# Filling the unused rows of the expert pages block by block, by copies in memory, in one attention, shared-FFN and MoE kernel

## The chip, the cores and the metric

One core of a Trainium2 chip runs the whole program. The metric is the device time of one execution in microseconds, as the median of several executions. The engines are TensorE (PE, with its weight loads PEld), VectorE (DVE), ScalarE (ACT), GpSimd (POOL) and SyncE (SP); transfers are issued by SP and POOL and carried out by 16 DMA engines.

## What is computed

The reference, cut to what matters (4096 tokens of width 512, all float32):

```
x = x + layernorm(linear_attention(layernorm(x), w_qkv, b_qkv, w_out, b_out))   # 16 heads, chunks of 128, decaying state
h = layernorm(x)
probs = softmax(h @ router.T); top 2 of 8 experts, weights renormalised
moe    = sum over e of combine[:, e] * (silu(h @ gate_e.T) * (h @ up_e.T)) @ down_e.T     # inner width 352
shared = sigmoid(h @ shared_gate.T) * ((silu(h @ g.T) * (h @ u.T)) @ d.T)                 # inner width 1408
out = x + layernorm(moe + shared)
```

The kernel computes only the two chosen experts of each token. It gathers tokens by expert for that.

## The kernel before, in words

**Stages.** The 4096 tokens are 8 blocks (`NB`) of 512 (`TOK`), each of 4 chunks (`NC`) of 128 rows. Phase 1 (to about 1360 us) runs attention, normalisation and routing of block after block and puts the shared FFN of earlier blocks between its pieces. Phase 2 (to about 1970 us) runs the experts. Phase 3 runs the last block of the shared FFN and the final normalisation. Matrix products are done as three passes on split operands (high and low parts), by the helper `three` (L728 to L730).

**Expert pages.** Tokens go to memory as rows of `xs_d` (`x1_normed_by_expert`): 39 pages (`NG`) of 256 rows (`GT`), each row 514 float32 (`DX`), 2056 bytes: the 512 normalised values, the combine weight and the token's number. A page belongs to one expert and is opened when a block needs it, so pages are used in order of time. The rows of a page that no token takes must hold an unused row: zeros, weight 0 and the number of a spare row. These patterns lie in two SBUF tiles `unused_row`, which are `xn2[:, 2]` and `xn2[:, 3]`, the same memory that later holds the normalised chunks 2 and 3 of each block.

**The fill before.** POOL issues 13 pieces `("zf", 0, i)` in block 0, each of 3 pages as two transfers (L563) from `unused_row`. Each piece first waits until TensorE has done the score product S of chunk i // 4, group i % 4. The first piece also clears a tail of `ffn_out` (L560). Two places wait for all the fills: the scatter `("sc", 0)` on POOL, and the ScalarE piece `("LX", 0, 1)` (L970), which overwrites the SBUF tiles.

**The scatter.** In each block a, after the routing ranks are known (piece RK), POOL issues 8 indirect transfers (L581) that put 128 rows each at their places in `xs_d`. Phase 2 gathers 128 rows at a time from it (L597).

**What sets the order.** Pieces of each block have hand-set places in `PLACES` and `OPENING`; block a adds `PERIOD` (44) times a, and `attention_offsets` returns them. `schedule` sorts them and puts the parts of the shared FFN between them: from place 60 on (`FILL_FROM`) each placed piece adds `max(1, passes)` to what was given, and an FFN part goes in whenever what was given lies behind an aim that grows evenly with the place. Each engine then runs its own pieces of this one list in order (`ORDER`), and waits on counters of finished pieces of the others. SP issues in order too: it loads `x` for the residual (xr, L665), attention weights (wa, L678), shared-FFN weights (raw, L690) and the transposed activations (xti, L700). POOL issues the stores x1o (L568, into `out`), xto (L572), sho (L592), and the scatter. xr for chunk 2 waits for the store x1o of chunk 0, since they share a tile.

Of the kernel before, what the change touches and what calls it, by code (L numbers as in the profile page):

```python
# [16 lines left out]
P = 128  # L17
# [4 lines left out]
G = HEADS // GH  # L22
TOK = 512
NC = TOK // P
NB = 8
SEQ = 1024
NCH = NB * NC
E, I_MOE, I_SH = 8, 352, 1408
# [14 lines left out]
GT = 256  # L43
NG = (2 * NB * TOK + E * (GT - 1)) // GT
SUB = GT // P
# [3 lines left out]
PART = [s for g in range(NG) for s in range(SUBS[g])]  # L49
FULLS = [sum(n == SUB for n in SUBS[:g]) for g in range(NG + 1)]  # L50
NJ = len(GROUP)
NZ = NG // 3
ZROWS = NG * GT // NZ
GU = 2 * I_MOE
DT = 3
DROWS = (P, P, I_MOE - 2 * P)
# [7 lines left out]
DX = D + 2  # L64
# [66 lines left out]
def attention_offsets(a):  # L131

    s = []
    for kind, places in PLACES.items():
        if a == 0:
            places = OPENING.get(kind, places)
        if a == 0 and kind == "xto":
            continue
        shape = ARGS.get(kind, (len(places),) if len(places) > 1 else ())
        for args, at in zip(itertools.product(*(range(n) for n in shape)), places):  # L140
            s.append((at, (kind, a, *args)))
    if a == 0:
        for i in range(NZ):
            s.append((20 + 8 * (i // G) + i % G, ("zf", a, i)))
    return s


# [91 lines left out]
def schedule():  # L239
# [70 lines left out]
    for q in range(LAST, NCH):  # L310
# [14 lines left out]
ORDER = {e: [p for p in PIECES if e in PARTS[p[0]]] for e in "PAVSG"}  # L325
PLACE = {e: {p: i + 1 for i, p in enumerate(ORDER[e])} for e in "PAV"}
# [32 lines left out]
def build(nc, x, w_att, w_ffn, w_gu, w_dn, w_router, b_qk, b_v, b_out, t_mask, t_dq, t_dk, t_lam, t_blk, t_ident,  # L359
# [6 lines left out]
    xs_d = nc.dram_tensor("x1_normed_by_expert", [NG * GT, DX], F32, kind="Internal").ap()  # L366
# [3 lines left out]
    with ExitStack() as ctx:  # L370
# [3 lines left out]
        def sem(name):  # L374
            return ctx.enter_context(nc.semaphore(name))
# [27 lines left out]
        def ffn_small(scope, tag):  # L403
# [18 lines left out]
        xin = sb("x_in", [NC, D], scope=phase1)  # L422
# [36 lines left out]
        cnt, pages, new, cum, page_end, page_base, away, fresh, had, had_end = (sb(n, [E], scope=phase1) for n in (  # L459
            "count", "pages", "pages_new", "pages_cum", "page_end", "page_base", "page_away", "page_fresh", "pages_had",  # L460
            "pages_had_end"))
# [6 lines left out]
        unused_row = [xn2[:, 2 + i, :] for i in range(SUB)]  # L468
# [56 lines left out]
        xt_out = sem("xT_out")  # L525
        xt_in = [sem(f"xT_in{k}") for k in range(KT)]
        xt_used = sem("xT_used")
        xs_zero, acc_zero, unused_id = sem("x1_by_expert_zero"), sem("ffn_out_zero"), sem("unused_row_id")
        second_weight = sem("second_weight")
        xs_out = [sem(f"x1_by_expert_out{i}") for i in range(NC)]  # L530
        sh_out = [sem(f"shared_out{i}") for i in range(2)]
# [20 lines left out]
        def pool_piece(pool, kind, *args):  # L552
            if kind == "zf":
                a, i = args
                pool.wait_ge(p_piece, done("P", "S", a, *divmod(i, G)))
                if i == 0:
# [1 line left out]
                    pool.wait_ge(unused_id, SUB)  # L558
                    tail = acc_d[(NB - 1) * TOK:, :].rearrange("(n p) d -> p n d", p=P)
                    pool.dma_start(out=tail, in_=unused_row[0][:, 0:D].unsqueeze(1).to_broadcast([P, NC + SUB, D])).then_inc(acc_zero, 16)  # L560
                rows = xs_d[i * ZROWS:(i + 1) * ZROWS, :].rearrange("(n s p) d -> s p n d", p=P, s=SUB)
                for k in range(SUB):
                    pool.dma_start(out=rows[k], in_=unused_row[k].unsqueeze(1).to_broadcast([P, ZROWS // GT, DX])  # L563
                                   ).then_inc(xs_zero, 16)
            elif kind == "x1o":
                a, c = args
                pool.wait_ge(v_piece, done("V", "L", a, c // 2))
# [6 lines left out]
            elif kind == "sc":  # L574
                a, = args
                pool.wait_ge(v_piece, max(done("V", "RK", a), done("V", "SM4", a)))
                if a == 0:
                    pool.wait_ge(xs_zero, 16 * SUB * NZ)
                for k in range(2):
                    for c in range(NC):  # L580
                        pool.indirect_dma_start(  # L581
# [356 lines left out]
        def act_attention(act, piece):  # L938
# [11 lines left out]
            elif kind == "N1":  # L950
                c, = args
                act.wait_ge(v_piece, done("V", "N1B", a))
                op = act.activation(xin[:, c, :], xin[:, c, :], ACT.Identity, bias=nshift[:, c:c + 1],
                                    scale=nrstd[:, c:c + 1])
            elif kind == "LN":
                h, = args
                act.wait_ge(v_piece, done("V", "LO", a, h))
                for i in range(2):
                    op = act.activation(o[:, i, :], o[:, i, :], ACT.Identity, bias=oshift[:, i:i + 1],
                                        scale=orstd[:, i:i + 1])  # L960
            elif kind == "LX":
                h, = args
                act.wait_ge(v_piece, done("V", "L", a, h))
                if (a, h) == (0, 1):
                    act.wait_ge(acc_zero, 16)
                    act.wait_ge(xs_zero, 16 * SUB * NZ)
                for i in range(2):
                    if a:
                        act.wait_ge(xs_out[2 * h + i], 32 * a)
                    op = act.activation(xn2[:, 2 * h + i, 0:D], x1[:, i, :], ACT.Identity, bias=lshift[:, i:i + 1],  # L970
                                        scale=lrstd[:, i:i + 1])
            elif kind == "W":
                u, = args
                act.wait_ge(wr_in[u % WAR], 16 * (u // WAR + 1))
                if u >= WAS:
                    act.wait_ge(p_piece, done("P", *last_use(a, u - WAS)))
                    act.wait_ge(ws_out[u % WAS], 32 * (u // WAS))
                op = act.copy(wa_hi[:, u % WAS, :], wa_raw(u))
            elif kind == "QK":
                m, = args  # L980
                dst = qT if m < G else kT
                if a and m == 0:
                    act.wait_ge(p_piece, done("P", "S", a - 1, NC - 1, G - 1))
                    act.wait_ge(v_piece, done("V", "KT", a - 1, NC - 1))
                op = act.activation(dst[:, m % G, :], b, ACT.Identity, bias=bqk[:, m:m + 1])
            elif kind == "Z":
                c, g = args
                if (c, g) == (0, 0):
                    act.wait_ge(a_piece, done("A", "QK", a, G - 1))
                if 4 * c + g >= 2:  # L990
                    act.wait_ge(p_piece, done("P", "S", a, *divmod(4 * c + g - 2, G)))
                for j in range(GH):
                    r = slice(j * HD, (j + 1) * HD)
                    op = act.copy(qz[r, g % 2, j, :], qT[r, g, c * P:(c + 1) * P])  # L994
            elif kind == "IP":
                c, half = args
                if half == 0 and c > 0:
                    act.wait_ge(p_piece, done("P", "OUT", a, c - 1))
                elif half == 0 and a:
                    act.wait_ge(p_piece, done("P", "OUT", a - 1, NC - 1))  # L1000
                op = act.copy(oT_hi[:, 2 * half:2 * half + 2, :], chunked(b[:, 0:2 * P]))  # L1001
            elif kind == "R1":
                op = act.copy(lgT[0:2 * R, :], b[0:2 * R, :])
            elif kind == "SM1":
                act.wait_ge(v_piece, done("V", "SM1", a))
                act.activation(sm["z"][:, :, :], lg[:, :, E:R], ACT.Exp, scale=-1.0)
                op = act.activation(sm["e"][:, :, :], sm["d"][:, :, :], ACT.Exp)
# [611 lines left out]
```

## Time and profile before

| | |
|---|---|
| median of 3 runs | 2072.4 us (2069.81 to 2073.74) |
| the profiled execution's own time | 2071.72 us |
| its span in the profile | 2069.9 us |
| PE busy / PEld busy | 1924.6 us (93%) / 1560.1 us (75%) |
| DVE / ACT / POOL busy | 1212.6 / 960.5 / 433.8 us |
| DMA | 389.26 MB, mean 188 GB/s |
| chain that ended last | PE 57%, DVE 6%, DMA 3%, ACT 2% |

The profile gives the span of one execution; 1.8 us of its time lie around the span. The chain that ended last is followed back from the last instruction. PE takes by far the most of it, so the places where PE stands idle, and for whom, decide what an edit outside PE is worth.

### The profile page before, as it was taken

To read this page: it belongs to the slowest core of one execution; us is meant where nothing else is said; L and a number is where in the kernel's file an instruction comes from. 1 tells how busy PE (TensorE), PEld (TensorE's weight loads), DVE (VectorE), ACT (ScalarE), POOL (GpSimd) and SP (SyncE) were. 2 spreads that over 40 slices of the span, in tenths; PEclk is the share of its full clock that TensorE was granted. 3 is DMA by queue.
4 is the path that set the end of the run, shared out by engine and by line. 5 is a ranking of instruction groups with operands and counts; after the bars stand their busy time and mean duration, and the time that the engine had idled before them with its cause. 6 is when DMAs were issued, how large, how long until landed. Compare 5 with 4: busy or idle time off the path is not lost.

```text
span 2069.9 us, 28246 instructions
## 1 busy us (share of the span) xinstructions
PE 1924.6 (93%) x10000; PEld 1560.1 (75%) x10000; DVE 1212.6 (59%) x2874; ACT 960.5 (46%) x1928; POOL 433.8 (21%) x444
## 2 busy tenths in 40 slices
PE   6788999899989999999999999999999999999996
PEld 5566677677767777767777777777998989899875
DVE  4555664574665574574575555664666666666466
ACT  4333343443443443443354334344666666666453
POOL 2301001001001001101000100120455555555222
PEclk9889999999999999999999999999999999999999
DMA  8976246336246337326435334565888988888597
GB/s 279 365 253 207 64 133 231 118 106 224 93 156 208 113 109 242 132 96 214 156 106 199 131 120 143 166 224 173 220 245 247 249 245 239 258 239 244 121 274 179
DMA packets 138378, 389.26 MB, mean 188 GB/s; under 512 B 16944, under 2 KB 17088, under 8 KB 131328
## 3 DMA queue, kind: packets, MB, share of 16 engines
q0 software_dynamic: 50256, 204.91, 33.4%
q1 hardware_dynamic: 87552, 182.49, 27.0%
q8 instruction: 81, 1.33, 0.3%
q14 instruction: 57, 0.47, 0.1%
q10 hardware_dynamic: 432, 0.07, 0.0%
HBM read 281.87 MB, written 105.53 MB: 187 GB/s over the span
## 4 chain that ended last, share of the span: by engine, by line
PE 57%; DVE 6%; DMA 3%; ACT 2%; issue 2%; SPq 1%; POOL 1%; DVEq 0%; ACTq 0%; POOLq 0%
PE banks L728 17%; PE banks L730 16%; PE banks L729 16%; PE banks L795 2%; PE banks L916 1%; DMA moe_dn_raw<-w_dn,w_index 1%; PE banks L922 1%; DMA xT_lo<-xt_scratch 1%; PE banks L809 1%; PE banks L802 1%; PE banks L815 1%; DMA ffn_w_raw<-w_ffn 1%; DVE ffn_gate_up_lo L1376 0%; PE banks L761 0%; SPq L700 0%
## 5 line engine op out<-in xcount | busy, mean ns | idle before, releaser
L728 PE MATMUL banks<-xT_hi,ffn_gate_up_hi 128*128 128x512 f32 x704 | 297.9, 423 | 14.6 <-DMA xT_lo<-xt_scratch 6.2
L730 PE MATMUL banks<-xT_hi,ffn_gate_up_lo 128*128 128x512 f32 x704 | 278.7, 396 | 0.0
L729 PE MATMUL banks<-xT_lo,ffn_gate_up_hi 128*128 128x512 f32 x704 | 278.2, 395 | 0.0
L728 PE MATMUL banks<-moe_gu_hi,moe_xT_hi 128*128 128x352 f32 x592 | 204.8, 346 | 3.0 <-DVE moe_xT_lo L1400 3.0
L994 ACT COPY q_one_head<-qT 32x128 f32<-32x128 f32 x512 | 151.0, 295 | 104.2 <-PE banks L795 98.9
L1393 DVE TENSOR_TENSOR moe_gu_lo<-moe_gu_raw,moe_gu_hi 128x704 fp32r<-128x704 f32 x156 | 135.3, 887 | 97.7 <-ACT moe_gu_hi L1051 97.7
L730 PE MATMUL banks<-moe_gu_hi,moe_xT_lo 128*128 128x352 f32 x592 | 191.2, 323 | 0.0
L729 PE MATMUL banks<-moe_gu_lo,moe_xT_hi 128*128 128x352 f32 x592 | 190.5, 322 | 0.0
L728 PEld LDWEIGHTS banks<-xT_hi,ffn_gate_up_hi 128*128 128x128 f32 x704 | 134.8, 191 | 59.9 <-issue 12.7
L633 POOL DMA_INDIRECT ffn_out<-moe_y,moe_x x74 | 119.2, 1610 | 201.0 <-ACT moe_y L1077 201.0
L729 PEld LDWEIGHTS banks<-xT_lo,ffn_gate_up_hi 128*128 128x128 f32 x704 | 135.0, 192 | 31.6 <-issue 6.7
L730 PEld LDWEIGHTS banks<-xT_hi,ffn_gate_up_lo 128*128 128x128 f32 x704 | 134.3, 191 | 29.7
L1376 DVE TENSOR_TENSOR ffn_gate_up_lo<-ffn_w_raw,ffn_gate_up_hi 128x768 fp32r<-128x768 f32 (+1 forms) x176 | 120.7, 686 | 57.6 <-ACT ffn_gate_up_hi L1024 57.4
L568 POOL DMA_DIRECT2D out<-x x32 | 17.5, 552 | 595.5 <-DVE x_shift L1116 595.2
L728 PE MATMUL banks<-ffn_down_hi,hidden_hi 128*128 128x512 f32 x308 | 132.8, 431 | 4.0 <-DVE hidden_lo L1386 3.9
L1001 ACT CAST attT_hi<-banks 128x256 fp32r<-128x256 f32 x64 | 23.6, 369 | 240.3 <-PE banks L809 240.2
L795 PE MATMUL banks<-q_one_head,kT 128*128 128x512 f32 x256 | 131.9, 609 | 0.7 <-ACT q_one_head L994 0.6
L1397 DVE TENSOR_TENSOR moe_dn_lo<-moe_dn_raw,moe_dn_hi 128x512 fp32r<-128x512 f32 x117 | 77.2, 689 | 93.7 <-ACT moe_dn_hi L1057 93.5
L730 PE MATMUL banks<-ffn_down_hi,hidden_lo 128*128 128x512 f32 x308 | 120.8, 392 | 0.0
L729 PE MATMUL banks<-ffn_down_lo,hidden_hi 128*128 128x512 f32 x308 | 120.2, 390 | 0.0
L581 POOL DMA_INDIRECT x_normed_by_expert<-x_normed,pos_int x64 | 65.9, 1029 | 249.2 <-DVE pos_int L1345 230.9
L1051 ACT CAST moe_gu_hi<-moe_gu_raw 128x704 fp32r<-128x704 f32 x156 | 118.1, 781 | 0.0
(273 smaller groups left out, 4408.1 us busy)
## 6 DMA issues: line engine op xcount, KB each, us to landing
ffn_w_raw<-w_ffn SPq DMA_DIRECT2D x176, 384.0 KB, 3.2
att_w_hi<-att_w_split SPq DMA_DIRECT2D x112, 256.0 KB, 3.7
att_w_lo<-att_w_split SPq DMA_DIRECT2D x112, 256.0 KB, 4.5
x_normed_by_expert<-x_normed POOLq DMA_DIRECT2D x26, 771.0 KB, 18.2
x_in<-x SPq DMA_DIRECT2D x32, 256.0 KB, 4.8
x<-x SPq DMA_DIRECT2D x32, 256.0 KB, 5.4
out<-x POOLq DMA_DIRECT2D x32, 256.0 KB, 2.7
fin_ffn_out<-ffn_out SPq DMA_DIRECT2D x32, 256.0 KB, 8.5
```

The lines of the kernel that those rows point to most:

```text
L581: pool.indirect_dma_start(out=xs_d[:, :], out_offset=bass.IndirectOffsetOnAxis(ap=posi[:, NC * a + c, k:k + 1], axis=0), in_=xn2[:, c, :], ...
L633: pool.indirect_dma_start(out=acc_d[:, :], out_offset=bass.IndirectOffsetOnAxis(ap=xg[:, j % XG, D + 1:DX].bitcast(I32), axis=0), in_=y[:, ...
L728: pe.matmul(out_ap, l_hi, r_hi, start=start, stop=False)
L729: pe.matmul(out_ap, l_hi, r_lo, start=False, stop=False)
L730: return pe.matmul(out_ap, l_lo, r_hi, start=False, stop=stop)
L795: mm = pe.matmul(b, kT[:, g, c * P:(c + 1) * P], qz[:, g % 2].rearrange("p h t -> p (h t)"), start=True, stop=True)
L994: op = act.copy(qz[r, g % 2, j, :], qT[r, g, c * P:(c + 1) * P])
L1001: op = act.copy(oT_hi[:, 2 * half:2 * half + 2, :], chunked(b[:, 0:2 * P]))
L1051: op = act.copy(gu_hi[:, i % 2, k, :], rgu[:, i % 2, k * GU:(k + 1) * GU])
L1376: op = ve.tensor_tensor(wgu_lo[:, n % WGU, gu_cut], src, wgu_hi[:, n % WGU, gu_cut].bitcast(F32), ALU.subtract)
L1393: op = ve.tensor_tensor(gu_lo[:, i % 2, k, :], rgu[:, i % 2, k * GU:(k + 1) * GU], gu_hi[:, i % 2, k, :].bitcast(F32), ALU.subtract)
L1397: op = ve.tensor_tensor(dn_lo[:, i % 2, k, :], rdn[:, k * D:(k + 1) * D], dn_hi[:, i % 2, k, :].bitcast(F32), ALU.subtract)
```

## The change

All 39 pages are no longer filled in block 0. Block 0 fills 12 of them from SBUF: the last page (38), which serves as the pattern, and pages 0 to 10. `PAGES[a]` is the number of pages that can be open after block a: 11, 15, 19, 23, 27, 31, 35, 38. Each later block a gets one new POOL piece `("zc", a)` at place 50, which issues a single transfer within memory: page 38, repeated, to the pages from `PAGES[a-1]` to `PAGES[a]` (4 pages; 3 in block 7). The scatter of block a waits for it. The fill pieces are 5 now, at places 20, 24, 28, 32 and 36, and piece i waits for the score product i as before.

```
-NZ = NG // 3
-ZROWS = NG * GT // NZ
+PAGES = [min(NG - 1, ((a + 1) * 2 * TOK + E * (GT - 1)) // GT) for a in range(NB)]
+FILLS = [range(NG - 1, NG)] + [range(q, min(q + 3, PAGES[0])) for q in range(0, PAGES[0], 3)]
...
     if a == 0:
-        for i in range(NZ):
-            s.append((20 + 8 * (i // G) + i % G, ("zf", a, i)))
+        for i in range(len(FILLS)):
+            s.append((20 + 4 * i, ("zf", a, i)))
+    else:
+        s.append((50, ("zc", a)))
...
-                rows = xs_d[i * ZROWS:(i + 1) * ZROWS, :].rearrange("(n s p) d -> s p n d", p=P, s=SUB)
+                rows = xs_d[FILLS[i][0] * GT:(FILLS[i][-1] + 1) * GT, :].rearrange("(n s p) d -> s p n d", p=P, s=SUB)
                 for k in range(SUB):
-                    pool.dma_start(out=rows[k], in_=unused_row[k].unsqueeze(1).to_broadcast([P, ZROWS // GT, DX])
+                    pool.dma_start(out=rows[k], in_=unused_row[k].unsqueeze(1).to_broadcast([P, len(FILLS[i]), DX])
                                    ).then_inc(xs_zero, 16)
+            elif kind == "zc":
+                a, = args
+                if a == 1:
+                    pool.wait_ge(xs_zero, 16 * SUB * len(FILLS))
+                pages = PAGES[a] - PAGES[a - 1]
+                rows = xs_d[PAGES[a - 1] * GT:PAGES[a] * GT, :].rearrange("(n r) d -> n r d", r=GT)
+                pool.dma_start(out=rows, in_=xs_d[(NG - 1) * GT:, :].unsqueeze(0).to_broadcast([pages, GT, DX])).then_inc(xs_copied, 16)
...
                 if a == 0:
-                    pool.wait_ge(xs_zero, 16 * SUB * NZ)
+                    pool.wait_ge(xs_zero, 16 * SUB * len(FILLS))
+                else:
+                    pool.wait_ge(xs_copied, 16 * a)
...
                 if (a, h) == (0, 1):
                     act.wait_ge(acc_zero, 16)
-                    act.wait_ge(xs_zero, 16 * SUB * NZ)
+                    act.wait_ge(xs_zero, 16 * SUB * len(FILLS))
```

## Rows read from the trace of the kernel before

**Rows 1.** The page: span and engine totals.

```profile
span 2069.9 us, 28246 instructions
PE 1924.6 (93%) x10000; PEld 1560.1 (75%) x10000; DVE 1212.6 (59%) x2874; ACT 960.5 (46%) x1928; POOL 433.8 (21%) x444
```

**Rows 2.** Windows of the opening: busy by engine, PEclk, DMA share, GB/s.

```profile
45.00:107.00 62.00, 48.17 (x267) 32.87 (x268) 36.13 (x89) 23.38 (x69) 20.45 (x29) 0.89 1.03 365
...
107.00:125.00 18.00, 13.73 (x89) 10.10 (x87) 12.58 (x36) 6.70 (x15) 0.50 (x1) 0.91 0.97 342
```

**Rows 3.** Waits of PE over the whole run: us, times, longest.

```profile
PE banks L802 <- DVE probsT L1245: 32.7, 14, 5.1
...
PE banks L728 <- DMA xT_lo<-xt_scratch: 6.2, 10, 2.7
```

**Rows 4.** The fill line L563: issue time in ns, first and last start, landing.

```profile
L563 POOL DMA_DIRECT2D x_normed_by_expert<-x_normed x26: 744/756/763, 45.4 to 106.7; - x26
...
DMA to landing us min/median/max: 12.0/18.2/22.0
```

**Rows 5.** POOL's timeline in the opening: start, us, operation, idle before.

```profile
99.41 1.11 POOL L568 DMA_DIRECT2D out<-x  x2
```

**Rows 6.** SP's timeline and SP's waits in the opening.

```profile
69.22 52.86 SPq L665 DMA_DIRECT2D x<-x  x4
...
SPq L665 <- DMA out<-x: 21.8, 2, 21.5
```

**Rows 7.** Timelines of DVE, ACT and PE where fills could be waited for.

```profile
92.65 1.29 DVE L1271 TENSOR_TENSOR x<-projected,x 128x512 f32<-128x512 f32 x2 [0.88 <-ACT projected L959]
...
130.65 1.30 DVE L1271 TENSOR_TENSOR x<-projected,x 128x512 f32<-128x512 f32 x2 [0.38 <-ACT projected L959]
...
136.13 1.51 ACT L970 ACTIVATE x_normed<-x,x_shift,x_rstd 128x512 f32<-128x512 f32 x2
...
66.46 1.01 PE L802 MATMUL banks<-q_decayed,state 128*128 128x128 f32 x4 [4.57 <-DVE probsT L1245]
130.41 0.77 PE L728 MATMUL banks<-x_normedT_hi,att_w_hi 128*128 128x512 f32 x1 [5.17 <-DVE x_normedT_lo L1224]
```

**Rows 8.** POOL's timeline where the copies will stand.

```profile
248.88 1.16 POOL L568 DMA_DIRECT2D out<-x  x2 [55.67 <-DVE x_shift L1116]
...
338.58 1.45 POOL L581 DMA_INDIRECT x_normed_by_expert<-x_normed,pos_int  x1 [25.54 <-DVE pos_int L1345]
...
602.58 0.54 POOL L592 DMA_DIRECT2D ffn_out<-shared_staged  x1 [0.29 <-ACT shared_staged L1043]
627.35 1.07 POOL L568 DMA_DIRECT2D out<-x  x2 [24.24 <-DVE x_shift L1116]
...
1246.47 0.54 POOL L592 DMA_DIRECT2D ffn_out<-shared_staged  x1 [1.54 <-ACT shared_staged L1043]
...
1299.53 1.46 POOL L581 DMA_INDIRECT x_normed_by_expert<-x_normed,pos_int  x1 [28.48 <-DVE pos_int L1345]
```

**Rows 9.** Windows behind copies 1 and 3 (columns as rows 2).

```profile
249.00:291.00 42.00, 40.54 (x225) 31.79 (x226) 27.05 (x61) 20.17 (x44) 1.04 (x2) 0.96 0.26 82
...
603.00:645.00 42.00, 38.53 (x175) 31.31 (x176) 21.66 (x60) 16.91 (x29) 2.26 (x5) 0.96 0.66 221
```

**Rows 10.** Loads of shared-FFN weights: SP and ACT timelines, and the page's landing.

```profile
253.43 6.96 SPq L690 DMA_DIRECT2D ffn_w_raw<-w_ffn  x2
...
269.24 0.41 ACT L1021 CAST ffn_gate_up_hi<-ffn_w_raw 128x256 fp32r<-128x256 f32 x1
...
ffn_w_raw<-w_ffn SPq DMA_DIRECT2D x176, 384.0 KB, 3.2
```

**Rows 11.** Weights of block 4's first product: load, landing, first use.

```profile
614.55 0.33 SPq L678 DMA_DIRECT2D att_w_hi<-att_w_split  x1
...
att_w_lo<-att_w_split SPq DMA_DIRECT2D x112, 256.0 KB, 4.5
...
L728 PE MATMUL banks<-x_normedT_hi,att_w_hi x32: 392/396/505, 621.3 to 650.3; 128*128 128x512 f32 x32
```

More of the change, by code:

```diff
@@ L527, in build @@
         xt_used = sem("xT_used")
-        xs_zero, acc_zero, unused_id = sem("x1_by_expert_zero"), sem("ffn_out_zero"), sem("unused_row_id")
+        xs_zero, xs_copied, acc_zero, unused_id = sem("x1_by_expert_zero"), sem("x1_by_expert_copied"), sem("ffn_out_zero"), sem("unused_row_id")
         second_weight = sem("second_weight")
```

2 rows, old and new, of the table PARTS are left out of this document.

## The prediction

> **What bounds the kernel now.** I first read the page's totals: PE is busy for 1924.6 of 2069.9 us, 93% [rows 1]. So an edit to transfers pays only where it shortens one of PE's idle stretches, and costs only where it makes one. The sum below is made against this execution: 2069.9 us of span and 1.8 us around it, 2071.7; the median of the runs shown is 0.7 above that.
>
> Next I read the windows of the opening. From 45 to 107 us the DMA share is 1.03 at 365 GB/s, and it stays at 0.97 to 125 us [rows 2]: the 39 pages are poured out here and every other transfer queues with them. In the same window PE is busy for 48.2 of 62 us. It looks as if the fills starve it. The list of PE's waits decides that: PE waits mostly for VectorE's masked probabilities (32.7 us in 14 waits), and the only transfer that it names is the transposed activations, 6.2 us in 10 waits [rows 3], none of them before 370 us. So I looked behind VectorE and ScalarE for a hidden transfer, below.
>
> **Part 1: fewer fills in block 0.** 26 transfers of 384 rows become 10: two of 128 rows, six of 384, two of 256. The removed pages are 39 - 12 = 27. A page is 256 x 2056 B = 0.526 MB, so 14.2 MB leave the opening; at 365 GB/s that is 39 us of full DMA. On POOL 26 x 756 ns = 19.7 us of issuing [rows 4] fall to at most 10 x 756 ns = 7.6 us, and POOL stands idle around them, so that is worth nothing by itself. The first 12 pages still wait for the products S of chunk 0 and the first of chunk 1, as they did, so the queues are full until about 75 us and much emptier after that. What was late because of it:
> - The store x1o of chunk 0 is issued at 99.41 [rows 5]. SP's next residual load waits for it, for 21.5 us [rows 6], which is landing behind the queued fills. That will shrink to a few microseconds, since nothing is queued ahead of the store any more. Who waits for SP there? VectorE's residual sum of the second pair starts at 130.65, and the row says that ScalarE's normalised projection released it, not the load [rows 7]. Gain 0.
> - The residual loads of the first pair, issued at 69.22 [rows 6], take up to 21.8 us, to about 92; the sum that reads them starts at 92.65, released by ScalarE [rows 7]. It is covered by about half a microsecond only. Gain 0, and a margin becomes large.
> - ScalarE's L970 at 136.13 must wait for all fills. The last was issued at 106.7 and lands at most 22 us later [rows 4], by 129; the row shows no idle time before it [rows 7]. Gain 0.
> - PE's idle stretches of 4.6 us before 66.46 and 5.2 us before 130.41 [rows 7] end on VectorE, which was at work on split weights and on the statistics of a normalisation.
>
> The bound from one side is 0. From the other, if these stretches were transfers after all: 4.6 + 5.2 = 9.8 us. I take 0, since each releaser named has just finished in its row.
>
> **Part 2: seven copies in memory.** Copies 1 to 6 write 4 pages, 2.1 MB, copy 7 writes 3. They write 14.2 MB in all, so nothing is saved in bytes written, and as much is now read from memory too. On POOL the issue cost is bounded by rows of the same kind: 756 ns for 384 rows [rows 4], 555 ns each for 128 rows [rows 5], so about 0.8 ns a row more and 1.3 us for 1024 rows, at most 2 us if it goes as whole fills (1024/384 x 756 ns). Seven times 1.3 us is 9 us on an engine with 50 us of idle time at each of these places [rows 8]. Cost 0.
>
> How long a copy runs has no row. The nearest is the fill, with the same row size and target: 2.1 MB at 365 GB/s [rows 2] is 5.8 us. If reading from memory costs as much again, 11.5 us. Those are the ends when all 16 engines share it; on four engines they are 23 and 46 us. I take 23 us for the reason given in the second rival.
>
> What each length meets:
> - The scatter waits for the copy. Copy 1 is issued at 249.9 and the scatter at 338.58: 88 us. The tightest is copy 7, 1247.0 to 1299.53: 52 us [rows 8]. Even 46 us fits.
> - POOL's transfers queued behind it: after copy 1 the next stands more than 50 us later. Behind copy 3 (issued at 603.1) the store x1o follows at 627.35 [rows 8], just past 23 us. Its reader is SP's residual load of the next block, some 50 us later. Copy 1's own wait for the fills is met by 129 us.
> - Shared-FFN weight loads run beside every copy. One issued at 253.43 is used at 269.24, 15.8 us later, and lands in 3.2 us [rows 10]. Twice or three times 3.2 us is still covered. DMA share behind copy 1 is 0.26 [rows 9], so there is room.
> - Attention weights of block 4 stand behind copy 3, where the share is already 0.66 [rows 9]. The pair is issued at 614.55 and 614.92, lands 4.5 us later, at 619.4, and PE uses it at 621.3 [rows 11]. Margin 1.9 us: this is the only thin cover that I found, and all other copies lie away from such loads. I take +0.5 us.
>
> **Part 3: the order.** The copy piece stands at places 94 and more, past the point where the FFN's planner counts, and adds one pass each time. Worked through the planner's rule, this moves ten pieces, among them ST of chunks 1 and 3 in block 3, one score product in block 6 and the down products 20, 27 and 40; each goes one FFN part (12 passes of some 0.24 us, 2.8 us) earlier or later. PE's work is the same. The bound for all is some 4 us either way, about one of the longer waits for the masked probabilities [rows 3]; value 0.
>
> **Sum.** 2071.7 + 0 (opening) + 0.5 (copy 3) + 0 (order), about 2072.
>
> **The rivals.**
>
> *The opening was bound by transfers (faster).* For it: the queues were full for 80 us, two covers there are as thin as half a microsecond, and the opening's PE is the idlest of phase 1. Against it: no releaser is a transfer. If a third to all of the 9.8 us come back, it gives 2062 to 2068; I put it at 2067. A lucky shift of the order ends there too. Chance 0.17.
>
> *Copy 3 takes the weights of block 4 (slower).* The transfer's outermost dimension is the 4 pages, not 128 partitions as in the fills. If the engines are dealt out along it, four of 16 carry a page each for 23 us or more, and any load spread over all 16 ends when those four let it. Place: 614.55 to 621.3, eight loads of 256 KB [rows 11]. Alone they need 2.1 MB at 365 GB/s, 5.8 us; on engines shared by halves 11.5 us, so the last comes 5.8 us later and the first by about 1.5. Price: up to 5.8 less the margin of 1.9, about 4 us, and some 4 more if at 46 us the copy also meets the loads after 627. It decides if copy 3 still runs 11.5 us after its issue. Result 2076 to 2080; with the spread of the order, 2077. Against it: later loads have their own margins, and it happens once. Chance 0.14.
>
> The Trainium skill, page "DMA: Bandwidth & Descriptors", section on why a DMA increments its semaphore by 16, says that the number of DMA engines is the largest one up to 16 that divides the slowest dimension of both sides, and its rules for kernel authors warn of a leading zero-stride broadcast of c copies, which keeps a transfer on at most c engines. By it each copy runs on four engines (three in block 7). No row of this trace shows such a shape. With copies of 23 us by it the sum stays 2072; with 5.8 us, for all 16 engines, it would be 2071.7.
>
> *The change does not do what it says.* The copies could run longer than 52 us (for example on one engine: 2.1 MB at 23 GB/s, 92 us), so that the scatter and POOL behind it wait. The scatter's landing is needed again only by the next block's normalised rows and, in block 7, by phase 2 near 1360 us. That gives 2072 to 2090. Chance 0.03.
>
> **How the numbers follow.** About 0.2%, or 4 us, is what a measurement of this kernel can tell from no change. Forecast, no visible change: 0.66. Slower by more: 0.14 + 0.03 = 0.17. Faster by more: 0.17. The forecast's own range is 2068 to 2076. The range 2066 to 2078 takes in the milder half of both rivals.
>
> **What would show it.** Right if the profile after has 10 transfers at L563's line instead of 26, a DMA share from 80 to 125 us well below 1, SP's wait of 21.5 us gone, and still the same PE stretches before 66.5 and 130.4 us and phase 2 at the same time. The copy's landing tells the engines: 6 to 12 us for 16, 23 to 46 for four. The first rival is right if PE starts block 1's first product well before 130 us. The second is right if PE's waits show attention weights near 621 us. I would be wrong altogether if a shared-FFN weight load or a scatter shows up as a releaser on PE's path.

## Result, and the profile after

The changed kernel takes 2095.6 us (median of 5 runs, 2093.36 to 2100.43), the kernel before 2073.6 us beside it (5 runs): ratio 1.0107, 95% interval 1.0093 to 1.0121. It is 22 us slower, where 2072 was forecast and 2078 was the upper end. The profiled execution is the longest of the five (2100.43 us), so its trace shows some 5 us more than the median.

The page after, span and engine totals, against [rows 1]:

```profile
span 2098.6 us, 28244 instructions
PE 1934.7 (92%) x10000; PEld 1567.6 (75%) x10000; DVE 1213.2 (58%) x2874; ACT 960.5 (46%) x1928; POOL 426.5 (20%) x435
```

The span grew by 28.7 us and PE's busy time by 10.1, with as many instructions; the rest is new idle time.

**The opening is as forecast.** The windows of the opening after (same columns as [rows 2]), SP's wait for the store, and the two PE stretches of [rows 7]:

```profile
45.00:107.00 62.00, 47.26 (x259) 33.03 (x259) 33.91 (x84) 21.34 (x62) 8.50 (x13) 0.86 0.68 237
107.00:125.00 18.00, 13.72 (x83) 9.77 (x82) 13.54 (x39) 8.49 (x21) 0.00 (x0) 0.91 0.00 0
```

```profile
SPq L676 <- DMA out<-x: 1.5, 2, 1.0
```

```profile
66.40 1.19 PE L813 MATMUL banks<-q_decayed,state 128*128 128x128 f32 x4 [4.57 <-DVE probsT L1256]
...
132.65 0.77 PE L739 MATMUL banks<-x_normedT_hi,att_w_hi 128*128 128x512 f32 x1 [5.17 <-DVE x_normedT_lo L1235]
```

The DMA share falls from 1.03 to 0.68 and from 0.97 to nothing. SP's longest wait for the store falls from 21.5 us to 1.0. And PE stands idle for the same 4.57 and 5.17 us. The transfers were not what it waited for.

**The copies run as long as forecast.** The copy line L573, the page's issues, and the DMA queues in the window from 262 to 272 us, in the middle of copy 1 (queue and kind: packets, MB, share of 16 engines; POOL's transfers are q0, SP's q1):

```profile
L573 POOL DMA_DIRECT2D x_normed_by_expert<-x_normed_by_expert x7: 657/684/684, 252.2 to 1268.7; - x7
...
DMA to landing us min/median/max: 24.4/24.7/25.8
```

```profile
q0 software_dynamic: 30, 0.99, 22.9%
q1 hardware_dynamic: 354, 0.77, 22.1%
```

A copy lands after 24.7 us; 23 was taken. q0's share of 22.9% of 16 engines is 3.7 engines: the copy is on four. By this the rule of the Trainium skill that the prediction weighed, on how many engines a transfer gets (page "DMA: Bandwidth & Descriptors", section on why a DMA increments its semaphore by 16), agrees with the trace. A packet of the copy is 0.99 MB / 30 = 33 KB, which is 16 rows of 2056 bytes (32,896): the rows of a page are contiguous and were joined. Each of the four engines carries a page, 16 such runs.

**The loads beside the copies are where it failed.** SP and PE at copy 3 (timeline columns as in [rows 5]), and the issues of the window from 600 to 626 us:

```profile
606.70 0.68 POOL L573 DMA_DIRECT2D x_normed_by_expert<-x_normed_by_expert  x1
...
616.70 0.33 SPq L689 DMA_DIRECT2D att_w_hi<-att_w_split  x1
617.07 0.43 SPq L689 DMA_DIRECT2D att_w_lo<-att_w_split  x1
...
633.12 0.76 PE L739 MATMUL banks<-x_normedT_hi,att_w_hi 128*128 128x512 f32 x1 [9.54 <-DMA att_w_lo<-att_w_split]
```

```profile
x_normed_by_expert<-x_normed_by_expert POOLq DMA_DIRECT2D x1, 2056.0 KB, 24.5
...
att_w_lo<-att_w_split SPq DMA_DIRECT2D x4, 256.0 KB, 17.3
```

The weights of block 4, which landed in 4.5 us [rows 11], take 17.3. The copy ends at 606.7 + 24.5 = 631.2. The low half of the first pair, issued at 617.07, lands 15.8 us later, at 632.9, and PE, idle for 9.5 us, starts at 633.12. The stall costs more than its length. These are the window of 42 us from copy 3 on, against [rows 9], and the first 5.7 us after the stall:

```profile
607.00:649.00 42.00, 27.00 (x117) 21.23 (x116) 20.46 (x57) 14.58 (x26) 1.51 (x3) 0.88 0.53 187
...
633.10:638.80 5.70, 5.68 (x14) 4.44 (x14) 0.00 (x0) 0.19 (x1) 0.00 (x0) 0.50 0.26 100
```

PE's granted clock is 0.50 in the second row, the lower of its two levels (1.2 GHz), after the 9.5 us in which it did nothing. Its 14 products there start 0.43 us apart, those behind 639 us 0.235 apart: another 2.7 us, 12.2 in all.

The waits of PE and of ScalarE over the whole run (us, times, longest):

```profile
PE banks L813 <- DVE probsT L1256: 36.2, 15, 5.0
...
PE banks L739 <- DMA att_w_lo<-att_w_split: 9.5, 1, 9.5
PE banks L739 <- DVE state L1267: 8.6, 5, 2.6
...
PE banks L843 <- DVE xT_staged_lo L1235: 5.7, 1, 5.7
```

```profile
ACT ffn_gate_up_hi L1032 <- DMA ffn_w_raw<-w_ffn: 16.6, 7, 7.2
ACT ffn_gate_up_hi L1035 <- DMA ffn_w_raw<-w_ffn: 14.0, 6, 5.1
```

ScalarE's 30.6 us were 13.4 before (7.1 in 3 waits and 6.3 in 5). Between 1060 and 1380 us, where copies 6 and 7 stand, they are 17.2 us after and 0.4 before. Where PE's path shifts is read from POOL's xto stores, one in each block, and the first gather of expert weights. Their start, less that in the kernel before, in us:

| block | 1 | 2 | 3 | 4 | 5 | 6 | 7 | phase 2 |
|---|---|---|---|---|---|---|---|---|
| changed kernel | +2.7 | +2.5 | +14.6 | +14.6 | +15.1 | +25.0 | +27.3 | +29.5 |
| order alone (e2) | 0.0 | -0.1 | -1.2 | -1.2 | -1.4 | +4.1 | +5.3 | +6.0 |
| copies alone, four engines (e3) | +2.3 | +2.1 | +11.7 | +11.7 | +11.8 | +17.2 | +18.9 | +22.5 |
| copies alone, 16 engines (e12) | -1.5 | -1.8 | -1.8 | -1.7 | -1.8 | -1.2 | -2.7 | -0.2 |

Two steps: 12 us at block 3, the stall and the slower clock behind it, and 10 at block 6. The same kernel run twice (e6 and e12) differs by up to 3 us in such a row, so smaller shifts say nothing.

### The profile page after: what moved, and what is told of

The parts are those of the page before. It is cut to its first block, busy times and chain, and to the rows that moved or that the text cites. A ratio compares the mean times of both kernels' runs of the same rounds, so it can differ in the third digit from the quotient of the medians.

```text
span 2098.6 us, 28244 instructions
## 1 busy us (share of the span) xinstructions
PE 1934.7 (92%) x10000; PEld 1567.6 (75%) x10000; DVE 1213.2 (58%) x2874; ACT 960.5 (46%) x1928; POOL 426.5 (20%) x435
## 4 chain that ended last, share of the span: by engine, by line
PE 76%; DVE 11%; DMA 6%; ACT 3%; issue 3%; SPq 1%; POOL 1%; DVEq 0%; ACTq 0%; POOLq 0%
PE banks L739 21%; PE banks L741 20%; PE banks L740 20%; PE banks L806 4%; DMA xT_lo<-xt_scratch 2%; DMA ffn_w_raw<-w_ffn 2%; PE banks L820 2%; PE banks L826 2%; PE banks L813 1%; PE banks L927 1%; DMA moe_dn_raw<-w_dn,w_index 1%; DVE probsT L1256 1%; PE banks L933 1%; DVE pair_stats L1133 1%; PE banks L772 1%
## 5 line engine op out<-in xcount | busy, mean ns | idle before, releaser
L577 POOL DMA_DIRECT2D out<-x x32 | 17.9, 561 | 627.9 <-DVE x_shift L1127 627.9
L739 PE MATMUL banks<-x_normedT_hi,att_w_hi 128*128 128x512 f32 x256 | 106.4, 415 | 19.7 <-DMA att_w_lo<-att_w_split 9.5
## 6 DMA issues: line engine op xcount, KB each, us to landing
x_normed_by_expert<-x_normed_by_expert POOLq DMA_DIRECT2D x6, 2056.0 KB, 24.6
```

Source lines behind the costliest of these rows:

```text
L739: pe.matmul(out_ap, l_hi, r_hi, start=start, stop=False)
```

## The experiments

All are timed against the kernel before on the same chip (its medians there: 2074.3, 2074.0, 2073.4, 2074.0 and 2075.0). All seven copies stand where the change put them unless it is said otherwise. "Old order" means that the planner doesn't count the copy pieces, so that the rest of the list is that of before.

| | median us | ratio | 95% interval |
|---|---|---|---|
| e1 changed order, 16 engines, runs of 4112 B | 2076.7 | 1.0015 | 1.0004 to 1.0026 |
| e2 kernel before with the changed order | 2079.6 | 1.0024 | 1.0010 to 1.0039 |
| e3 old order, copies as changed | 2090.7 | 1.0080 | 1.0061 to 1.0099 |
| e4 old order, 16 engines, 4112 B | 2076.5 | 1.0012 | 1.0000 to 1.0024 |
| e5 old order, two copies of half rows | 2078.2 | 1.0023 | 1.0012 to 1.0035 |
| e6 old order, 16 engines, 32,896 B | 2070.0 | 0.9982 | 0.9970 to 0.9995 |
| e7 old order, as changed, at place 30 | 2191.1 | 1.0567 | 1.0543 to 1.0591 |
| e8 old order, 16 engines, 4112 B, at place 30 | 2116.7 | 1.0208 | 1.0188 to 1.0228 |
| e9 old order, columns split 512 + 2 | 2080.8 | 1.0040 | 1.0026 to 1.0054 |
| e10 changed order, 16 engines, 32,896 B | 2076.2 | 1.0005 | 0.9993 to 1.0017 |
| e11 e12, with all 39 pages filled in block 0 too | 2072.1 | 0.9996 | 0.9987 to 1.0005 |
| e12 e6 once more | 2072.5 | 1.0000 | 0.9989 to 1.0012 |
| e13 old order, two copies at each place | 2096.2 | 1.0113 | 1.0091 to 1.0134 |
| e14 e12's shape, two copies at each place | 2076.9 | 1.0013 | 1.0002 to 1.0024 |
| e15 changed kernel, copy 3 alone on 16 | 2088.0 | 1.0068 | 1.0051 to 1.0085 |
| e16 changed kernel, all but copy 3 on 16 | 2089.4 | 1.0075 | 1.0062 to 1.0088 |
| e17 old order, copies twice as long on four | 2159.5 | 1.0407 | 1.0387 to 1.0427 |

**Order against shape: e1 to e4.** The edits, alone or together:

```
-            given += max(1, passes([piece]))                       # old order; the same in the total
+            given += 0 if piece[0] == "zc" else max(1, passes([piece]))
...
-                rows = xs_d[...].rearrange("(n r) d -> n r d", r=GT)      # four engines
+                rows = xs_d[...].rearrange("(n p s) d -> p n (s d)", p=P, s=GT // P)
+                page = xs_d[(NG - 1) * GT:, :].rearrange("(p s) d -> p (s d)", s=GT // P)
+                pool.dma_start(out=rows, in_=page.unsqueeze(1).to_broadcast([P, pages, GT // P * DX])).then_inc(xs_copied, 16)
```

e2 is the kernel before, with empty copy pieces that are counted.

> The changed kernel with the same seven copies, but with 128 as the outermost dimension of both sides, as the fills have it. Theory A (few engines: a copy sits on four of 16 for 24.6 us, and every load that is spread over 16 lands only when those four let it): a copy lands in 6 to 12 us, the stall of 9.5 us before block 4's first product is gone, and the time falls from 2095.6 to 2074 to 2080. Theory B (the planner's shifted order): 2090 to 2096 still, since the order is the changed one. Theory C (traffic within memory slows the loads whatever engines carry it): a copy of some 10 us, 2085 to 2095.

> The kernel before with all 39 pages filled in block 0, plus the seven pieces at place 50, which issue nothing: the planner's order is that of the changed kernel, and nothing else is. Theory A: 2072 to 2077, the order costs at most a few microseconds. Theory B: 2085 to 2095.

> The changed kernel with its copies as they are, but the planner does not count them, so all other pieces stand as in the kernel before. Theory A: 2090 to 2096, all or nearly all of the loss is still there. Theory B: 2073 to 2078.

> Both mended: copies over 16 engines and the planner's old order. Theory A: 2071 to 2076, level with the kernel before, because the opening was not bound by its transfers. If the opening relief were worth something after all: below 2069.

Measured: the same bytes to the same places in the same order cost 18.9 us more in the changed shape (2095.6 against 2076.7 for e1; in the old order 2090.7 against 2076.5). The landing of a copy falls from 24.6 us to 11.8 (e1), that of the residual loads that start some 11 us behind its issue from 14 or 15 us to 4.2 (e4), since the copy is then all but over. The order has a price of its own: e2 against before 5 us, the changed kernel against e3 4.9 us; but e1 against e4, the same pair of orders with 16 engines, shows 0.2. By the table of shifts e2 loses it in block 6. PE's waits between 985 and 1112 us in e2 hold two that the kernel before lacks in that block:

```profile
PE banks L804 <- DVE probsT L1247: 2.6, 1, 2.6
...
PE banks L797 <- ACT shared_staged L1045: 1.4, 1, 1.4
```

So a piece moved by one FFN part uncovers chains on VectorE and ScalarE that the FFN hid. The shape makes most of the loss, the order at most the rest.

**Engines or length of a run: e5, e6 and e9.** e6 takes `p=16` in place of `p=P`, so that 16 engines carry runs of 32,896 bytes. e5 and e9 split the columns, so that rows aren't contiguous and can't be joined:

```
+                page = xs_d[(NG - 1) * GT:, :].unsqueeze(0).to_broadcast([pages, GT, DX])
+                for cols in (slice(0, DX // 2), slice(DX // 2, DX)):      # e9: slice(0, D), slice(D, DX)
+                    pool.dma_start(out=rows[:, :, cols], in_=page[:, :, cols]).then_inc(xs_copied, 16)
```

> Planner's old order, copies still on four engines (the pages outermost), but in two transfers of half rows, 1028 B a piece, so that contiguous rows can't be merged into long runs. In the changed kernel a page of 526,336 B in 24.6 us on one engine is 16 runs of 32,896 B of 1.54 us each, if rows are merged. Theory A1 (few engines: whatever lies behind the copy on the four engines waits for it): copy 25 to 30 us, 2088 to 2092 as in the run with four engines and the old order. Theory A2 (long runs: an engine serves the queues in turn, one run against one row of 2 KB, so a load with 8 rows per engine waits 8 x 1.54 = 12.3 us): residual loads beside a copy land in 4 to 8 us instead of 14, and the time is 2075 to 2079.

> Planner's old order, the same runs of 32,896 B as in the changed kernel, but 16 of them outermost, so that each engine carries four. Theory A1: a copy lands in 6 to 12 us, 2075 to 2079. Theory A2: the same copy length, and a load beside it waits at most for four runs, 6 us, so 2075 to 2079 as well; only loads that stand within 6 us of the copy's issue land late, in 8 to 10 us.

> Old order, four engines, copies split by columns: one transfer with rows of 2048 B (the 512 values) and one with the last two columns, 8 B a row. The run with half rows put its two transfers on the engines side by side and a load beside them still landed with the copy's end, so it left open whether length of run or number of engines holds the loads. Here nearly all bytes are in one transfer on four engines. Theory A1 (whatever lies behind or beside the copy on those engines comes out with the copy's end, whatever its runs): main copy 24 to 30 us, residual loads beside it 13 to 16 us, time 2086 to 2092. Theory A2 (turns between queues, one long run against one short row): residual loads 4 to 8 us, time 2075 to 2080.

e6 says that long runs by themselves cost nothing at this place: a copy is over in 10.2 us, four runs an engine. Its lead over before did not hold in e12 (1.0000), so I take it as chance. e5 lies between and decides less: its two halves go side by side (q0 is at 48.5% of 16 engines between 416 and 426 us, so on eight), residual loads land in 9.9 us, the weights of block 4 in 14.0, and PE stands 5.9 us at 626.9. (The row of that stall names VectorE, but the low half of the first pair, issued at 614.5, lands 12.1 us later, at 626.6.) e9 did not make the shape that it was meant to: the page's issues give

```profile
x_normed_by_expert<-x_normed_by_expert POOLq DMA_DIRECT2D x6, 2048.0 KB, 10.3
...
x_normed_by_expert<-x_normed_by_expert POOLq DMA_DIRECT2D x6, 8.0 KB, 32.0
```

2 MB in 10.3 us are not four engines' work, although the pages are outermost here too, and why is not shown; but the 8 KB of the last two columns, 1024 rows of 8 bytes, take 32 us, and loads beside them are late (residual 9.1 us, weights 13.5). It says how dear tiny rows are, nothing on the question, which e5 and e9 leave open.

**Another place: e7 and e8.** The copy piece at place 30 in place of 50, on four engines and on 16.

> Planner's old order, copies as in the changed kernel, but at place 30 of each block instead of 50, so that copy 3 runs before and not beside the load of block 4's attention weights. If the loss was mostly that one meeting: the 7.8 us stall before block 4's first product is gone and the time falls from 2090.7 to 2078 to 2083; what is left is late shared-FFN weights. If every copy costs about the same wherever it stands: 2088 to 2093.

> Planner's old order, 16 engines with runs of 4112 B, at place 30. Both theories: level with the same kernel at place 50, 2072 to 2077. Below 2071 only if the opening relief pays and the 2 us that are left at place 50 come from where the copies stand.

Both missed, far on the other side. POOL issues the copy right behind the scatter, at 193.9, and SP issues the eight loads of the output weights from 195.0 on, in every block. PE's waits in e7 and in e8:

```profile
PE banks L739 <- DMA att_w_lo<-att_w_split: 107.5, 6, 19.9
```

```profile
PE banks L740 <- DMA att_w_lo<-att_w_split: 34.8, 6, 6.7
```

That is one meeting with a weight load, measured six times: 17.9 us of PE with the copy on four engines and 5.8 us on 16. The expectation had looked at POOL's idle time there, not at what SP loads next.

**The opening and the whole: e10, e11 and e12.** e10 is the changed kernel with e6's copy, e12 is e6 again. e11 adds to e12 all fills of before in block 0:

```
-FILLS = [range(NG - 1, NG)] + [range(q, min(q + 3, PAGES[0])) for q in range(0, PAGES[0], 3)]
+FILLS = [range(q, q + 3) for q in range(0, NG, 3)]
```

> The changed kernel with nothing else mended than the copy's shape (16 runs of 32,896 B per page outermost). If order and copy add up: the fastest form so far, 2070, plus what the shifted order costs, 2 to 5 us: 2072 to 2075. If 16 engines with 4112 B are as good: 2076 as that run gave.

> Old order, all 39 pages filled in block 0 as in the kernel before, and the seven copies on 16 engines with long runs as well (they write the same again). Against the same kernel with 12 pages filled this leaves only the relief of the opening. If the relief is worth nothing, as predicted: 2069 to 2074, level within 2 us with the kernel beside it. If it is worth something: 3 to 10 us slower than that.

> The same kernel as the one with 16 engines and long runs before, beside the two above: again 2068 to 2073, slightly below the kernel before; if the lead was chance, 2073 to 2077.

e11 and e12 differ by 0.4 us: fewer fills in block 0 are worth nothing that shows. Only the copy's shape mended (e10) gives 19.4 of the 22 us back; mended in the order of before (e12) it is level with the kernel before, and no kernel beats that in each of its runs.

**Copy 3 by itself: e15 and e16.** The copy takes one shape for `a == 3`, the other for the rest.

> The changed kernel with copy 3 alone spread over 16 engines, the other six as they were. If the stall on block 4's weights is what copy 3 costs, some 12 us come back of 2095.6: 2083 to 2085, and what is left (some 8 us over 2076.2) lies at copies 6 and 7. If most of the loss comes from the shared-FFN weights at all copies, less than 4 us come back: 2092 or more.

> The complement: the changed kernel with the other six copies spread over 16 engines and copy 3 alone on four. If copy 3 costs 12 us by itself: 2076.2 + 12, 2087 to 2089. If the loss is spread over all copies: 2076 to 2080.

Alone on four engines, copy 3 costs 2089.4 - 2076.2 = 13.2 us, as expected. Alone mended it gives back 7.6 of the 19.4 (each median is good to some 3 us), less than the 12 expected and more than the 4 of the other case. The shifts at block 3 are clear (+11.2 in e16, +2.4 in e15); what follows in e15 is a wait of 6.2 us for VectorE's transposed activations and ScalarE's waits of 32.5 us for shared-FFN weights, 17.3 of them between 1060 and 1380 us, at copies 6 and 7. So copy 3 is the largest single part, some 8 to 13 us, and the other six cost 6 to 12 together.

**Turns, or held until the end: e13, e14 and e17.** The loads beside a copy landed near its end, so either an engine serves the queues in turns, with a load's rows between long runs, or a load waits until the copy is over. e13 and e14 issue a second copy, to the pages of the next block, right behind the first. e17 keeps one transfer but makes it twice as long, with two pattern pages and

```
+                m = 2 if a < NB - 2 else 1
+                rows = xs_d[PAGES[a - 1] * GT:(PAGES[a - 1] + m * pages) * GT, :].rearrange("(n r) d -> n r d", r=m * GT)
+                pool.dma_start(out=rows, in_=xs_d[(NG - m) * GT:, :].unsqueeze(0).to_broadcast([pages, m * GT, DX])).then_inc(xs_copied, 16)
```

> The old order, and at each of the seven places two copies on four engines, the second to the pages of the next block (none in block 7), so that those engines are busy for about 49 us in place of 24.6. A load that starts some 13 us into the first copy lands 14 to 15 us later with one copy. Theory A, an engine takes a run of each queue in turns: such a load has the same few rows to bring past the same long runs, so it still lands in 14 to 16 us, though copies go on for 35 us more; only the loads between 25 and 49 us are late in addition. Theory B, a load is held until the copies issued before it are done: it lands in 35 to 38 us. Time: A 2093 to 2110, B above 2120.

> The same doubled copies, but spread over all 16 engines (runs of 32,896 bytes), so some 20 us in place of 10. Theory A and B alike: each load that meets them is late by up to 10 us more than beside a single copy; both copies are over before or just as the loads that start 13 us later need their engines. 2072 to 2082. Above 2085 would say that the bytes copied, not the four engines, make the loss.

> The old order and one copy at each place, but copies 1 to 5 write eight pages, four destinations of two pages each, from two pattern pages: the outermost dimension is still 4, so four engines should carry 32 long runs each, some 49 us in place of 24.6 (two separate copies had gone to different engines side by side). Theory A, turns between long runs and a load's own rows: a residual load that starts 13 us into the copy still lands in 14 to 16 us, and the shared-FFN weights that start 4 us into it in 16. Theory B, held until the copy is over: 35 to 38 us and 45 us. Time: A 2095 to 2120, since the loads of the next 25 us are late too, B above 2130.

e13 did not do what it was to do. Its queues between 262 and 272 us:

```profile
q0 software_dynamic: 60, 1.97, 46.4%
```

Twice the packets and twice the share of the changed kernel (30 and 22.9%), 7.4 engines: the second copy ran on other engines beside the first, and both were over within 27 us. Loads beside them landed as before (residual 14.6 to 15.9 us), which fits both theories. e14's time came as expected: twice the bytes on 16 engines, the two copies over some 18 us after they are issued, cost 2.9 us. So it is not the bytes. But its loads are late too, as its issues from 413 to 425 and from 262 to 275 us show:

```profile
ffn_w_raw<-w_ffn SPq DMA_DIRECT2D x2, 384.0 KB, 16.4
...
x<-x SPq DMA_DIRECT2D x2, 256.0 KB, 9.9
```

Long runs on 16 engines hold up a load as those on four do, while they last. Four engines make one copy last 24.6 us in place of 10, and the loads that start 10 us and more into it, block 4's weights above all, then still meet it.

e17 tells the two apart. SP's timeline beside copy 1, which POOL issues at 251.66, and ScalarE's waits for the weights:

```profile
255.09 6.93 SPq L702 DMA_DIRECT2D ffn_w_raw<-w_ffn  x2
262.12 0.85 SPq L677 DMA_DIRECT2D x<-x  x2
271.20 4.24 SPq L702 DMA_DIRECT2D ffn_w_raw<-w_ffn  x2
```

```profile
270.86 0.41 ACT L1033 CAST ffn_gate_up_hi<-ffn_w_raw 128x256 fp32r<-128x256 f32 x1
...
283.38 0.83 ACT L1036 CAST ffn_gate_up_hi<-ffn_w_raw 128x768 fp32r<-128x768 f32 x1 [1.32 <-DMA ffn_w_raw<-w_ffn]
...
299.27 0.40 ACT L1033 CAST ffn_gate_up_hi<-ffn_w_raw 128x256 fp32r<-128x256 f32 x1 [12.82 <-DMA ffn_w_raw<-w_ffn]
```

The landings of the loads one by one, from the issues of narrow windows (issue plus landing), the copy ending at 251.7 + 46.2 = 297.9:

| load | issued | landed | after the one before |
|---|---|---|---|
| shared-FFN weights | 255.1 | 270.7 | |
| shared-FFN weights | 261.7 | 283.4 | 12.7 |
| residual x, first | 262.1 | 294.9 | 11.5 |
| residual x, second | 262.6 | 298.3 | 3.4 |
| shared-FFN weights | 271.2 | 299.3 | 1.0 |

A load held until the copy is over could not land at 270.7 and 283.4. In turns it can, and the queues in the window from 282 to 286 us show the turns themselves (packets, MB, share of 16 engines):

```profile
q0 software_dynamic: 13, 0.43, 24.8%
q1 hardware_dynamic: 13, 0.02, 1.5%
```

There are thirteen runs of the copy and thirteen packets of SP's loads. Taken one by one, each of the four engines sends one packet of a load (0.08 to 0.12 us for a row) and then one run of the copy (0.248 x 16 x 4 us / 13 = 1.22 us), over and over, 1.30 to 1.34 us a turn. A load of 128 rows puts 8 rows on each engine, and behind them the trace has a packet of 4 bytes that takes a turn as well. On the last of the four engines this packet goes at 270.34, 282.87 and 294.45, right before the landings at 270.7, 283.4 and 294.9. Nine turns are 11.7 to 12.1 us; the distances measured are 12.7 and 11.5. As soon as the copy ends, the rest lands within 1.4 us.

So each load needs nine turns, and loads queue behind each other. The first shared-FFN weights, with nothing ahead of them, landed in 15.6 us, as theory A had it (16). The residual loads took 33 to 36 us, which is what theory B had given (35 to 38), because the weights ahead of them used up most of the copy's 32 turns. The time, 2159, is above both 2120 and 2130: a long copy builds a backlog, and the weights of block 4 in its path stop PE for 28.3 us at once. Neither the residual loads nor the time tell the theories apart; the two landings during the copy and the turns one by one do. The expectation for turns left the backlog out.

The Trainium skill, page "DMA: Bandwidth & Descriptors", section "Queues, rings and completion order", says that a DMA engine goes round the queues that have work for it and changes only when a whole packet is through. e17's trace agrees: its turns change at each packet, and the distances of 11.5 and 12.7 us follow from them. It also says that a packet holds several descriptors. e5's trace agrees: its rows of 1028 bytes go in packets of 4112, 0.165 us each. But nine turns of such a packet and a row of a load are 2.3 us, too little for residual loads of 9.9 us, so why short rows delay loads as well is not shown.

## Why the prediction was wrong

Its forecast, no visible change, is out. The terms of the sum that failed are those of the copies: +0.5 us for copy 3, and nothing for the shared-FFN weights beside the others. The second rival, "Copy 3 takes the weights of block 4", had the place and the four engines right, but a chance of 0.14 and a price of 4 us.

- *What bounds the kernel; the opening, value 0.* Right. SP's wait went, the PE stretches stayed, and e11 against e12 is level. The first rival ("bound by transfers") falls with it.
- *The copies: 23 us, four engines; POOL's issue and the scatter's cover, cost 0.* Right: 24.7 us on 3.7 engines, 0.68 us an issue; no scatter waits on PE's path.
- *"Engines shared by halves."* This is the step that failed. Halves were meant in bytes: a load lands in twice its time. The engine shares turns, and a turn of the copy is 32,896 bytes (1.22 us) while one of the load's 256 KB in 128 rows is 2048: the load gets 2 of 35 KB, 6% and not 50%. So a load's price is not a multiple of its own 4.5 us but nine turns of 1.3 us, about 12 us, plus what is queued ahead of it, and at most until the copy ends. At copy 3 the queue decides: two loads of shared-FFN weights are issued from 608.32 on, ahead of block 4's weights. Until the copy ends the four engines carry only their rows (3072 bytes) between the runs, and the first row of block 4's weights (2048 bytes) goes there at 631.1, when the other twelve engines have long brought their 768 of the 1024 rows. In place of +0.5 the trace shows a stall of 9.5 us and 2.7 us of slower clock; e16 measures 13.2 for copy 3 alone, e15 7.6. The prediction had no term for the clock.
- *"Twice or three times 3.2 us is still covered."* The same error, for the shared-FFN weights. The load that was used at 269.24 [rows 10] is now issued at 256.53 and used at 272.62, 16.1 us later, with 0.7 us of waiting: the margin of 15.8 was used up to the last. At copies 6 and 7 it was not enough, and ScalarE's waits rise by 17.2 us in all. "This is the only thin cover that I found" came out of the price: at 12 us a load, covers of 10 us are thin too. "DMA share behind copy 1 is 0.26, so there is room" took a mean over 16 engines for the state of each: with the copy on four, these four are busy with it alone for 92% of the time (22.9% of 16 are 3.7 of 4). By e15 and e16 the six other copies cost 6 to 12 us where the sum had 0. With copy 3 they are the 19.4 us between the changed kernel and e10.
- *The order: value 0, bound 4 us either way.* The bound was nearly right: +5 us (e2), +4.9 (the changed kernel against e3), +3.8 (e10 against e12), but +0.2 (e1 against e4). With medians that are good to some 3 us, the order costs 0 to 5 us, and 4.9 in the changed kernel itself. To bound it, the prediction named one score product in block 6 among the moved pieces; that is where e2 loses its time.
- *Chances.* The forecast took the copies as running 23 us on four engines, and the second rival asked only for a copy that still runs 11.5 us after its issue. So its condition was already part of the forecast, and 0.14 was too little for it. The sum with the measured terms: the copies' shape costs 14 us (e3 against e4) to 19 (the changed kernel against e10), the order 0 to 5, so 2072 becomes 2086 to 2096. Of the signs of being right, all on the opening came true; the one that failed was phase 2 at the same time, which is 29.5 us late.

## What to carry to other kernels

A transfer's shape decides not only how long it takes but what it does to every load beside it: ask for the number of engines and the bytes of one contiguous run, and price a neighbour by turns (its rows per engine and one more, times the time of one long run), plus the loads queued ahead of it, up to the end of the transfer. Put the broadcast dimension inside and one of 16 outside: the same copy is then over in 10 us and costs nothing at place 50, though at place 30, right before a weight load, 16 engines still cost 5.8 us a meeting (e8). And before placing background traffic, list the loads that start during its whole length, with their margins, rather than the idle time of the engine that issues it.

## What was not expected of the hardware

- A load spread over all engines lands 13 us later beside a copy on four (17.3 us in place of 4.5), although 12 engines are free: it ends with the slowest of its engines.
- Two four-engine copies issued one behind the other ran on different engines: 46.4% of 16 against 22.9% for one, both over within 27 us (e13).
- A copy within memory of 2.1 MB takes 10.2 us on 16 engines (206 GB/s written) and 24.6 on four (21.4 GB/s written by each); e1's runs of 4112 bytes take 11.8, so the length of a run matters little there.
- 1024 rows of 8 bytes take 32 us, three times as long as the 2 MB beside them (e9).
- Where two queues share an engine, one packet of each goes in turn: a row of 0.08 to 0.12 us, then a run of 1.22 us (e17).
- After 9.5 us without work PE runs the next 5.7 us at a granted clock of 0.50 (the changed kernel, 633.1 to 638.8 us).
- Open: why the short rows of e5, on eight engines and over within 20 us, still make residual loads land in 9.9 us. A four-engine copy in short runs was meant in e5 and e9, and neither made it.
